# Block attention's queries computed with the weights moving and turned by small transposes, and a new order of the first layers' pieces

## The reference, cut to what matters

```python
def _L1_xattn_ref(hidden_states, encoder_hidden_states, attention_mask, Wq, Wk, Wv, Wo):
    pooled = x.reshape(B, nb, BLOCK, D).mean(axis=2)            # BLOCK = 16, nb = 16
    q = (pooled @ Wq).reshape(B, nb, KV, HPG, DH)               # Wq is 256 x 1024
    k = (encoder_hidden_states @ Wk).reshape(B, Lenc, KV, DH)
    v = (encoder_hidden_states @ Wv).reshape(B, Lenc, KV, DH)
    scores = jnp.einsum('bngqd,blgd->bgqnl', q, k) * SCALE
    ...
    out = jnp.einsum('bgqnl,blgd->bngqd', attn, v)
    out = out.reshape(B, nb, H * DH) @ Wo
```

## Time and profile before

| | |
|---|---|
| median of 3 runs | 4121.93 us (4109.13 to 4132.47) |
| the profiled execution: time / span | 4129.74 us / 4128.0 us |
| mean granted TensorE clock | 0.958 of full |
| PE busy | 3852.9 us (93%) |
| PEld busy | 2819.5 us (68%) |
| DVE busy | 2819.7 us (68%) |
| ACT busy | 2269.9 us (55%) |
| POOL busy | 2236.2 us (54%) |
| first layers | about 0 to 1130 us of the span |
| local layers | the rest, granted clock 1.00 from 1269 us to 3996 us |

### The profile page before, as it was taken

One profiled execution on the slowest core, in us unless ns is written; L12 is line 12 of the kernel. 1 busy time (PEld: TensorE's weight loads), 2 busy tenths in 40 slices (PEclk: granted clock), 3 DMA queues, 4 the chain that ended last, 5 costly groups with the idle time before them and its releaser, 6 DMA issues. The chain is left out here.

```text
span 4128.0 us, 76628 instructions
## 1 busy us (share of the span) xinstructions
PE 3852.9 (93%) x25848; PEld 2819.5 (68%) x25848; DVE 2819.7 (68%) x9145; ACT 2269.9 (55%) x6540; POOL 2236.2 (54%) x2090
## 2 busy tenths in 40 slices
PE   7789999897659999999999999999999999999996
PEld 5677777776426777777777777777777777777775
DVE  4677776665357777777777777777777777777762
ACT  2333433332236666666666667666666666666662
POOL 1555554555266556555655655565555556555630
PEclk8899998998789999999999999999999999999998
DMA  3655555556210001010001001010010101010000
GB/s 118 152 148 146 140 141 133 152 146 185 62 34 9 12 11 40 19 33 11 28 22 33 21 7 43 22 30 10 11 43 17 33 11 34 26 33 12 8 5 26
DMA packets 137360, 223.54 MB, mean 54 GB/s; under 512 B 24656, under 2 KB 98320, under 8 KB 135440
## 3 DMA queue, kind: packets, MB, share of 16 engines
q0 software_dynamic: 40960, 134.25, 12.4%
q1 hardware_dynamic: 96016, 84.41, 6.6%
HBM read 191.39 MB, written 2.10 MB: 47 GB/s over the span
## 5 line engine op out<-in xcount | busy, mean ns | idle before, releaser
L1555 PE MATMUL pj<-w_qkv,l_xT 128*128 128x512 f32 x2304 | 1061.1, 597 | 6.2 <-ACT l_qk_sq L1702 3.3
L1500 POOL TENSOR_TENSOR l_qk_rot<-l_qk_cos,l_qk_sin 128x512 f32<-128x512 f32 x384 | 561.3, 1462 | 850.5 <-DVE l_qk_sin L1810 566.4
L381 POOL DMA_INDIRECT f_rows<-in_emb,f_expert x512 | 508.2, 993 | 427.0 <-PE facc L598 219.2
L1555 PEld LDWEIGHTS pj<-w_qkv,l_xT 128*128 128x128 f32 x2304 | 412.7, 191 | 384.6 <-issue 370.3
L1715 ACT ACTIVATE l_probs<-l_probs,l_low 128x128 f32<-128x128 f32 x1536 | 594.0, 391 | 1.8
L1635 PE MATMUL pj<-l_xnT,l_w 128*128 128x256 f32 x2112 | 511.0, 387 | 9.3 <-PEq L1657 8.1
L1802 DVE TENSOR_REDUCE l_ss<-l_qk_sq 128x8 f32<-128x512 f32 x384 | 261.5, 681 | 330.6 <-ACT l_qk_sq L1702 176.9
L1828 DVE CUSTOM_DVE_ANT_0 l_probs<-sc,l_shut,l_r_q 128x128 f32<-128x128 f32 x1536 | 440.1, 343 | 55.5 <-PE tp L1594 45.8
L1681 ACT ACTIVATE l_qk_raw<-pj 128x512 f32<-128x512 f32 x384 | 227.0, 591 | 430.1 <-PE pj L1555 417.8
L1635 PEld LDWEIGHTS pj<-l_xnT,l_w 128*128 128x128 f32 x2112 | 383.5, 190 | 72.8 <-issue 23.0
L1618 PE MATMUL y_ps<-w_o,l_oT 128*128 128x256 f32 x1536 | 339.5, 379 | 4.0 <-ACT l_oT L1681 2.5
(11 more groups left out here) (308 smaller groups left out, 7224.2 us busy)
## 6 DMA issues: line engine op xcount, KB each, us to landing
w_qkv<-in_L_ffn_Wqkv SPq DMA_DIRECT2D x12, 1024.0 KB
l_w<-in_ff_w SPq DMA_DIRECT2D x6, 1408.0 KB, 6.1
f_rows<-in_emb,f_expert POOLq DMA_INDIRECT x512
w_o<-in_L_ffn_Wo SPq DMA_DIRECT2D x6, 1024.0 KB
w_qkv<-in_L_ffn_Wqkv SPq DMA_DIRECT2D x12, 512.0 KB
l_xs<-l_stream SPq DMA_DIRECT2D x48, 128.0 KB
l_xf<-l_stream SPq DMA_DIRECT2D x48, 128.0 KB
l_xs<-l_stream SPq DMA_DIRECT2D x48, 127.0 KB
```

Of the source, the lines that this page charges most:

```text
L381: pool.indirect_dma_start(rows[:, j % RH, k, :], None, dram["emb"], bass.IndirectOffsetOnAxis(ap=expert[:, n % 2, at:at + 1], axis=0)).the ...
L1500: pool.tensor_tensor(qk_rot[:, i % ROTS, :], qk_cos[:, b, :], qk_sin[:, b, :], ALU.add).then_inc(rotated if s == 0 else pool_front, 1)
L1555: last = pe.matmul(pj[b][:, :], xT[:, k, t * P:(t + 1) * P], w_qkv[:, k, s * INNER + c * 512:s * INNER + (c + 1) * 512], start=(k == 0), s ...
```

## The change

Three things, in `first_layers` alone.

1. `e_q` becomes three pieces. `e_w0` and `e_w1` keep the pooled rows stationary (128 x 16) and move 512 columns of the weights each; the result has the 16 blocks on partitions. DVE copies the first half (`e_w0`) and ACT the second (`e_w1`) into `e_flat`, a view of the first 16 partitions of `e_p`. The new `e_q` turns it by eight transposes of 16 x 128 into the layout that it had.
2. PE's list has two pieces more for each row, so the rotation of the banks shifts.
3. The table `ORDER` is new for all engines.

```diff
-        ("c_q0", -4), ("b_hT", -3), ("e_cT", -5), ("c_s0", -4), ("c_s1", -4), ("c_up10", -5), ("c_s3", -4), ("c_s2", -4), ("e_k", -5), ("a_v", -2),
+        ("c_q1", -4), ("c_up10", -5), ("c_s0", -4), ("c_s1", -4), ("e_k", -5), ("c_s2", -4), ("c_s3", -4), ("c_m0", -4), ("c_m1", -4), ("c_m2", -4),
...
-        ("b_ctx", -3), ("e_ctx", -4), ("e_mask", -4),
+        ("e_ctx", -5), ("e_mask", -4), ("b_ctx", -2),
...
+        e_flat = e_p[0:NB, :, :].rearrange("p g n -> p (g n)")
...
+            def e_w(i):
+                def queries(n):
+                    pe.wait_ge(loaded["e"], 16 * LOADS["e"])
+                    pe.wait_ge(e_pooled, n + 1)
+                    s = Slot(f"e_w{i}", n)
+                    wait(pe, s.taken, s.before)
+                    for k in range(KC):
+                        last = pe.matmul(s.bank[0:NB, :], pooled[:, k, :], e_wq[:, k, i * 512:(i + 1) * 512], start=(k == 0), stop=(k == KC - 1))
+                    last.then_inc(ps_full, 1)
+                return queries
+
             def e_q(n):
-                pe.wait_ge(loaded["e"], 16 * LOADS["e"])
-                pe.wait_ge(e_pooled, n + 1)
+                copied("e_w0", n)
+                copied("e_w1", n)
                 s = Slot("e_q", n)
                 wait(pe, s.taken, s.before)
                 for c in range(8):
-                    for k in range(KC):
-                        last = pe.matmul(s.bank[:, c * NB:(c + 1) * NB], e_wq[:, k, c * P:(c + 1) * P], pooled[:, k, :], start=(k == 0), stop=(k == KC - 1))
+                    last = pe.transpose(s.bank[:, c * NB:(c + 1) * NB], e_flat[:, c * P:(c + 1) * P], ident[0:NB, 0:NB])
                 last.then_inc(ps_full, 1)
...
+                "e_w1": copy_of("e_w1", e_flat[:, 512:1024], "e_pT", 512, NB),
...
-                wait(dve, ps_full, last_before("e_hT", n, "e_q"))
+                wait(dve, ps_full, last_before("e_hT", n, "e_w0 e_w1"))
...
+                       "e_w0": copy_of("e_w0", e_flat[:, 0:512], "e_pT", 512, NB),
```

More of the change, by code:

```diff
@@ L59, in first_layers @@
     ORDER["tensor"] = [
[6 rows of a table removed]
-        ("c_up7", -4), ("e_v", -5), ("c_up8", -4), ("a_q", -1), ("c_up9", -4), ("e_pT", -5), ("a_k", -1), ("e_o", -5), ("b_cT", -2), ("e_y", -5),
-        ("c_hT", -3), ("a_z", -1), ("e_u", -5), ("c_q1", -3),
[6 rows of a table added]
+        ("e_s1", -5), ("c_up7", -4), ("c_up8", -4), ("a_k", -1), ("c_up9", -4), ("e_v", -5), ("e_cT", -4), ("e_pT", -5), ("a_q", -1), ("e_o", -5),
+        ("a_z", -1), ("e_y", -5), ("b_hT", -2), ("c_hT", -3), ("e_u", -5), ("c_q0", -3),
     ]
     ORDER["scalar"] = [
[6 rows of a table removed]
@@ L76, in first_layers @@
-        ("c_tanh9", -4), ("c_diag8", -4), ("a_hT", -1), ("c_diag9", -4), ("e_v", -5), ("e_exp", -5), ("a_q", -1), ("e_pT", -5), ("e_o", -5),
-        ("c_tanh10", -4), ("c_tanh11", -4), ("e_y", -5),
[6 rows of a table added]
+        ("c_diag8", -4), ("c_diag9", -4), ("b_cT", -2), ("e_exp", -5), ("e_v", -5), ("e_cT", -4), ("e_pT", -5), ("a_q", -1), ("e_o", -5),
+        ("c_tanh10", -4), ("c_diag10", -4), ("e_y", -5),
     ]
     ORDER["vector"] = [
[4 rows of a table removed]
-        ("a_norm", -1), ("c_coef3", -4), ("b_gt", -3), ("e_mask", -5), ("a_stats", 0), ("a_y", -2), ("c_dot4", -4), ("d_top", -5), ("c_coef4", -4),
[3 rows of a table removed]
@@ L88, in first_layers @@
-        ("e_probs", -5), ("b_add", -3), ("c_stats", -3), ("c_dot10", -4), ("c_dot11", -4), ("c_norm", -3), ("a_k", -1), ("c_coef10", -4), ("a_z", -1),
-        ("c_dot12", -4), ("e_u", -5), ("c_coef11", -4), ("f_stats", -5), ("c_coef12", -4),
[4 rows of a table added]
+        ("a_norm", -1), ("d_k", -5), ("b_scan", -3), ("c_m7", -4), ("c_dot3", -4), ("a_y", -2), ("c_coef3", -4), ("d_top", -5), ("b_gt", -3),
+        ("c_dot4", -4), ("d_inv", -5), ("b_stats", -2), ("c_coef4", -4), ("c_dot5", -4), ("d_o", -5), ("a_stats", 0), ("e_stats", -5),
@@ new lines, in first_layers @@
+        ("c_coef5", -4), ("b_qk0", -3), ("c_dot6", -4), ("e_norm", -5), ("c_coef6", -4), ("b_qk1", -3), ("b_qk2", -3), ("b_qk3", -3), ("e_hT", -5),
+        ("c_dot7", -4), ("b_h0", -3), ("e_mask", -5), ("c_coef7", -4), ("e_w0", -5), ("c_dot8", -4), ("b_h1", -3), ("c_coef8", -4), ("b_centre", -3),
+        ("c_dot9", -4), ("e_s", -5), ("c_coef9", -4), ("e_low", -5), ("b_spread", -3), ("b_norm", -2), ("e_probs", -5), ("b_add", -3), ("a_k", -1),
+        ("c_stats", -3), ("c_dot10", -4), ("c_coef10", -4), ("c_norm", -3), ("c_dot11", -4), ("c_dot12", -4), ("e_u", -5), ("f_stats", -5),
@@ L90, in first_layers @@
     ]
     ORDER["gpsimd"] = [
[3 rows of a table removed]
-        ("a_rstd", 0), ("f_rstd", -5),
[4 rows of a table added]
     ]
     ORDER["sync"] = [
-        ("b_ctx", -3), ("e_ctx", -4), ("e_mask", -4),
+        ("e_ctx", -5), ("e_mask", -4), ("b_ctx", -2),
     ]
@@ L726, in _ @@
                        "b_h0": b_h0, "b_h1": b_h1, "c_q0": c_q(0), "c_q1": c_q(1), "c_y0": c_y(0), "c_y1": c_y(1),
-                       "d_q": d_q, "d_k": d_k, "d_v": d_v, "d_s": d_s, "d_pT": d_pT_, "d_o": d_o, "e_cT": e_cT, "e_k": e_k, "e_v": e_v_, "e_q": e_q,
+                       "d_q": d_q, "d_k": d_k, "d_v": d_v, "d_s": d_s, "d_pT": d_pT_, "d_o": d_o, "e_cT": e_cT, "e_k": e_k, "e_v": e_v_, "e_w0": e_w(0), "e_w1": e_w(1), "e_q": e_q,
                        "e_s0": e_s(0), "e_s1": e_s(1), "e_pT": e_pT_, "e_o": e_o_, "e_y": e_y_, "e_u": e_u})
@@ L832, in _ @@
                 "e_cT": copy_of("e_cT", flat(ctxT_e[:, :, :]), "e_k e_v"), "e_k": copy_of("e_k", flat(e_kT[:, :, :]), "e_s0 e_s1"),
-                "e_v": copy_of("e_v", flat(e_v[:, :, :]), "e_o"), "e_q": copy_of("e_q", flat(e_qT[:, :, :]), "e_s0 e_s1", 8 * NB), "e_exp": e_exp,
+                "e_v": copy_of("e_v", flat(e_v[:, :, :]), "e_o"), "e_w1": copy_of("e_w1", e_flat[:, 512:1024], "e_pT", 512, NB), "e_q": copy_of("e_q", flat(e_qT[:, :, :]), "e_s0 e_s1", 8 * NB), "e_exp": e_exp,
                 "e_pT": copy_of("e_pT", e_pT[:, :, :, :].rearrange("p t g n -> p (t g n)"), "d_o e_o"), "e_o": copy_of("e_o", e_o[:, :], "e_y", 2 * 4 * NB),
@@ L1163, in _ @@
                        "d_k": copy_of("d_k", flat(k_ad[:, :, :]), "a_z d_s"), "d_top": d_top_, "d_inv": d_inv_, "d_o": d_o,
-                       "e_hT": e_hT, "e_mask": e_mask, "e_s": e_s, "e_low": e_low, "e_probs": e_probs, "e_u": add_tiles("e_u")})
+                       "e_hT": e_hT, "e_w0": copy_of("e_w0", e_flat[:, 0:512], "e_pT", 512, NB), "e_mask": e_mask, "e_s": e_s, "e_low": e_low, "e_probs": e_probs, "e_u": add_tiles("e_u")})
             gained = False
```

## The result

Median 4090.54 us (4086.45 to 4095.76, 4 runs) beside 4122.19 us (4109.13 to 4132.47, 4 runs) of the kernel before: ratio **0.9922**, 95% interval 0.9895 to 0.9948. That is 31.7 us less. The forecast was 18 less (4104), in a range of 4060 to 4148.

The account below looks back on a forecast made before the run. PE was taken as the bound, partly at half clock. Steps 5 to 9 at −1.3 each (−6.5), steps 10 and 11 −13.2, d_s −4, step 12 +2.4, step 3 +3.4 sum to −18 us: 4104, range 4060 to 4148.

Parts of the forecast that it names:

- step 3: First layers, step 3: b_cT and then a_q and a_k follow the load, so c_hT starts later, +3.4 us.
- step 4: First layers, step 4: an existing 8.8 us stop hides the delay from the load, so no change was counted.
- the signs that the text named: Right: PE idle 2 to 5 us before b_cT, copy within 0.5 us; wrong: half-clock as long, stop at e_w0/e_q.
- steps 10 and 11: Steps without a b_ctx load, so no new wait: −6.6 us each, −13.2 together, with no half-clock stretch.
- PE's own work, +0.4: PE at the queries: 3.75 us out, 3.6 plus 0.6 in, +0.4 us a full step; in step 12, +2.4.
- The wait for the copy, −2.2 a step: PE's stop before the scores for ACT's queries copy goes, covered by a_hT and b_cT: −2.2 us a step.
- The clock, −3.4, and given back, +2.0: Half clock around the queries goes, −3.4 us a step; the stop before b_cT gives back +2.0, bounds 0 and 3.4.
- The new wait, +3.3 (1.3 to 4.8): PE stands before b_cT for b_ctx's DMAs, landing 8.0 us behind b_h1: +3.3 us a step, steps 5 to 9.
- Other moves, −1.4 a step, and `d_s`, −4: Shorter waits at c_hT and before e_hT, −1.4 us a step; more work ahead of d_s, −4 us in all.
- the load decides: Rival, chance 0.20: late DVE makes the wait before b_cT 7.2 us and keeps half clock; slower, 4142 us.
- All of the gain: Rival, chance 0.22: loads land near 6 us, stop under 1.5, clock 1.00; −6.6 us in seven steps, 4074 us.
- Hidden: Rival, chance 0.18: PE's gain is lost at the next stop or the ring of gathers; 4122 us within 10.

Follow-up runs that it names:

- the new queries alone: Kernel before with e_w0, e_w1 and the new e_q but the old order of pieces: 4125.15 us, ratio 0.9969.
- the order alone: Changed kernel without e_w0 and e_w1, so the new order with the old e_q: 4112.28 us, ratio 0.9927 against the kernel before.
- the own load: Changed kernel with ctx_b loaded by its own transfer right behind the previous row's b_cT: 0.9826 against the kernel before, on another chip 0.9920.
- the late turn: Changed kernel with b_cT ahead of e_y again and its copy behind that of e_o: 4086.18 us, 0.986 against the kernel before.
- the doubled products: Kernel before with the queries' eight groups of four products issued twice, same result: 4099.96 us, ratio 1.0133.
- the quick chip: Third comparison's chip, where the kernel before had a median of 4047 us; the changed kernel measured 4031.94 us there, ratio 0.9965.
- the last two runs: Kernel before with only b_cT moved between a_hT and the scores, 1.0022; the same with its context loaded by its own transfer, 1.0014.

## Why the prediction was right, and where it was not

The direction and the range held, and the place did in part: all of the gain lies in the first layers. But the sum came out 14 us short, and several of its terms held only by offsetting each other. Steps 5 to 9 fell by 20 us more than my terms for them, step 3 came out 9 us the other way, and step 4 grew by 6.2 us that I had at nothing: that the sum lies in the range is in part luck.

Of the signs that the text named, the copy within 0.5 us of the eighth transpose came true, and so did the releaser of the stop ahead of `b_cT`. The stop was under the 2 to 5 us in four of five steps, steps 10 and 11 had half-clock stretches of 6.8 and 10.2 us at or behind the scores where none was expected, and one of the signs of being wrong came, a stop at `e_q` for its copies in these two steps.

*PE's own work, +0.4.* Measured +0.5 (1.89 + 1.89 + 0.67 = 4.45 in place of 3.9). Right. In step 12 the eight products took 6.50 us, and with two short stops and the transposes the new three came to 7.9 from the first `e_w0` to the end of `e_q`, where I had 9.4 and the old queries 6.98: +0.9 in place of +2.4.

*The wait for the copy, −2.2 a step.* It went from the kernel, as forecast, but I had read it wrongly. "The queries were ready later than their modelled end says" does not hold: on the chip without late pick-ups the same 32 products are copied 0.04 us behind their end, and on another chip eight transposes are copied up to 3.1 us late. It is ACT that picks them up late; the 7.63 us of the earlier trace rows carry "remote". Neither part alone takes that away: the copy is late in five of eight steps with the new queries alone and in two of eight with the order alone. With both it is on time in all eight, in the profile of after as with the own load and with the late turn, on chips where other pick-ups stay late. So the wait didn't go because `a_hT` and `b_cT` cover it, as I had it, but because the copy is no longer late at this place. Why is not shown.

*The clock, −3.4, and given back, +2.0.* Net −1.4 a step. The new stretch at half clock at the scores is 3.4 us in four of the five steps and absent in step 8, in line with what I took. The mechanism was half right: I hung the drop on the stop, but the doubled products bring one with no stop at all, and in the kernel before the drop was there first: the clock falls at 412.7, and PE stands from 414.3 to 417.35. And I counted the clock at this place alone, −13.8 us in all, where the half-clock time with PE busy fell by 66 us over all first layers, an estimated 33 us. In the kernel after, the stop ahead of `b_cT` with its transposes keeps 3.4 us, and with the own load these are gone. The Trainium skill, "TensorE: Matmul & The Clock Gate", Part 4: PE-mode transpose, says of a transpose that "it doesn't count as PE-busy the same way". By that, as the prediction used it, all 3.4 would have come back and the stretch stayed as long as it was; it is a third of that, so the trace does not agree with this use of the rule. The 15 us that the new queries are worth on the quick chip are nearly this term alone.

*The new wait, +3.3 (1.3 to 4.8).* Measured 1.80, 1.54, 1.79, 1.51 and 2.63 us in steps 5 to 9, mean 1.85. The stop, its place and its releaser were right. The landing was over-sized: `b_cT` starts 6.5 to 7.0 us behind `b_h1` in place of 8.0. What I left out is step 4: there the load held `b_cT` 10.6 us, at a place where I had let an older stop hide it, and the step grew by 6.2 us. SP issued the load only at 165.12, 6.7 us behind the end of `b_h1`, where in the full steps it does so 0.03 to 0.53 us behind it; its wait reads "remote", a late pick-up of SP's. On the quick chip SP is on time there and the stop is 4.7 us. With 3.3 in step 3 the load's stops make 23 us in this profile, and on the other chip, where they make 16.9, taking them away gave 18.

*Other moves, −1.4 a step, and `d_s`, −4.* **This is the step that failed.** The −1.4 was for `c_hT`, and was not worked out from a row; its stops fell by 0.9 a step (10.9 to 4.8 in seven). But in steps 5 to 8 those at `d_s` (14.4 us) and `c_up` (4.1) all went too, and PE's stops of over 0.5 us fall from 12.0 a step to 6.8, with the new wait counted in. I wrote that I expected as many of the late pick-ups after. In this profile there were fewer, 41 us on ACT in place of 73; but the own load and the late turn have 64 and 67 and gain more, so that is not the explanation by itself. The order alone, at 0.9927, was worth 30 us, where its terms (−2.2 for the copy among them, +3.3 for the load) made −9 (five times −0.3, twice −3.6, −4 and +3.4). Steps 5 to 9 together fell by 30.6 us, PE's busy time by 11.7 and its idle time by 18.9, where I had −6.5, or −10.5 with `d_s`.

*Steps 10 and 11, −6.6 each.* Step 10 fell by 4.5 us, all that follows it by 6.5. In these two steps the copies of `e_w0` and `e_w1` came late, and `e_q` stood 4.1 and 1.6 us for them. In step 11 that was the case that the text named as the cover that can go: `c_dot8` waited for a late gather, and ACT stood in `c_tanh8`. In step 10 it was DVE that stood 4.6 us ahead of its reader of `b_h0`, which PE had ended 6 us before.

*Step 3, +3.4.* Wrong in sign: −5.7 (`c_hT` at 79.91, before at 85.57). `b_h1` ended 7.1 us earlier, at 66.8, and the load landed 4.2 us behind it, not 8. The other kernels with the new order start the first `c_s0` at 86.5 to 91.8, those with the old order at 89.6 to 94.1, so a part of the 7 us ahead of it may be scatter.

Of the rivals, "the load decides" did not come: DVE was not late, and the stop stayed under 2.7 us in the steps that it spoke of, though it reached 10.6 in step 4. "All of the gain" (4074) was 16 us off, hardly more than the forecast; what it named, that every place where PE waited has more work ahead of it, fits the stops that went, but no run shows that this is why they went. "Hidden" is what happened to single moves in the old order, as the last two runs show, but not to the change as a whole.

**What stays open.** Why the order is worth 0.7% on one chip, while on the quick chip the changed kernel gains 15 us in all and its queries, measured with the own load, 15 us too. If the parts add, the order is worth about nothing where ACT picks its work up in time. But that they add was not tested: the order alone was not run there, and together with the own load, under the old queries, it is worth 17.5 us. Open too is what makes the copy of the queries late in the old order and not in the new. Nor is it settled which of its moves carries the gain: GpSimd's order and the turn's place don't, the places of `c` and `d` pieces on PE, DVE and ACT were not tried apart.

## What to carry to other kernels

A stop that PE shows ahead of one piece need not be the fault of the piece that it waits for: look whether its releaser was late for a reason of its own, and don't count on a single filled stop, which was worth nothing in two runs here. What pays is what takes PE's work or its half-clock time away, and a transfer that no longer stands behind a wait it doesn't need: one load split by its first reader gave more than the whole change had on the same chip (18 us beside 15). Look at the clock beside the stops: here it gave back more than the stops did. And a gain of under 1% in a kernel with such waits needs a second chip before its size is believed.

## What the chip showed that I had not expected

The same two kernels gave 0.9922 on one chip and 0.9965 on another. Behind the first layers the changed kernel took the same on both: 4085.8 − 1089.5 = 2996.3 us and 4032.6 − 1036.0 = 2996.6. All the difference is in the first layers, a full step of 118.4 us on the one, and on the other this window:

```profile
308.10:416.30 108.20, 105.67 (x552) 83.09 (x551) 90.01 (x370) 46.93 (x142) 71.40 (x71) 1.00 0.68 164
```

The step has as many PE records as that of the first chip (552) and 6.7 us less of PE's busy time, at a clock of 1.00 for 0.94. The first chip has about once a step a row like this one of the kernel after, on ACT, behind a piece that PE had ended at 370.3:

```profile
375.65 0.49 ACT L755 ACTIVATE f_e_pT<-fp 128x384 f32<-128x384 f32 x1 [5.08 <-remote]
```

What ACT waits for there is in none of the records; of the 8 such waits in the profile of after, 5 had no instruction fetch during them or in the 3 us ahead, which speaks against that cause; it was not tried. Behind this one PE stood 2.63 us ahead of `d_o`, and from 376.8 the clock was at half for 6.8 us, so such a wait can cost twice.

And 64 narrow products in a row, with 16 columns moving, took the clock down with PE not idle, and 32 of them with a stop of 1 us or less ahead, while eight of 512 columns and eight tiny transposes did not.
